# A fused attention and expert kernel on one core: both ends of the attention part re-ordered, and VectorE's first state difference put ahead of the mask of the first scores in every quad

## The reference, cut to what matters

```
xn = layernorm(x)
q, k, v = split(xn @ W_qkv)              # 16 heads of width 8; k is normalised per head
for each chunk of 64 tokens:
    inter  = S applied to q              # S is an 8 x 8 state per head and sequence
    scores = causal_mask(q k^T)          # 64 x 64 per head
    y      = inter + scores @ v
    S      = S + v^T k
out = x + y @ W_o + ffn(xn)              # ffn: the expert with the largest affinity, gated
```

## Time and profile before

| what | value |
|---|---|
| three runs | 389.06, 389.95, 390.57 us; median 389.95 |
| the profiled execution | 390.6 us, its span 388.9 us |
| mean granted TensorE clock | 0.987 of full speed |
| TensorE matmul busy | 357.8 us, 92% of the span |
| TensorE weight load busy | 300.1 us, 77% |
| VectorE, ScalarE, GpSimd busy | 288.6, 241.9, 251.4 us |
| attention part | 0 to about 243 us |
| expert part | from there to the end |

### The profile page before, as it was taken

The page is one execution under the profiler, slowest core; times in us unless marked ns, Lnnn a source line. Parts: engine busy times, 40 slices in busy tenths (PEclk is TensorE's granted clock), DMA queues, the critical chain, the costliest instruction groups (busy, mean ns, idle before and its releaser), DMA issues.

```text
span 388.9 us, 17635 instructions
## 1 busy us (share of the span) xinstructions
PE 357.8 (92%) x6900; PEld 300.1 (77%) x6900; DVE 288.6 (74%) x802; ACT 241.9 (62%) x657; POOL 251.4 (65%) x245
## 2 busy tenths in 40 slices
PE   7799999999999898999899988999999999999991
PEld 6477776766766666667567567899999999999990
DVE  8897895995966776857668458688888778877770
ACT  4788766766856556536545362666677676666760
POOL 3486757887875745445454350288888888888884
PEclk9999999999999999999999899999999999999996
DMA  6223153274022022443423423555555555555330
GB/s 193 56 57 83 35 166 111 79 227 138 10 78 78 25 86 70 106 149 98 132 67 109 139 63 79 136 70 74 69 72 68 72 67 73 72 72 71 35 28 0
DMA packets 55153, 33.18 MB, mean 85 GB/s; under 512 B 5352, under 2 KB 52768, under 8 KB 55072
## 3 DMA queue, kind: packets, MB, share of 16 engines
q1 hardware_dynamic: 42800, 23.53, 22.0%
q0 software_dynamic: 12272, 8.54, 15.7%
HBM read 18.72 MB, written 13.78 MB: 84 GB/s over the span
## 4 chain that ended last, share of the span: by engine, by line
PE 52%; issue 28%; POOL 12%; DVE 4%; ACT 2%; POOLq 1%; ACTq 0%; DVEq 0%
PE sc L1260 12%; POOL out_dram L494 12%; PE bank L1312 10%; PE bank L1321 4%; PE bank L1209 4%; PE bank L1196 4%; PE bank L1187 3%; PE bank L1292 2%; PE bank L1281 2%; PE bank L1241 2%; PE bank L1202 2%; PE bank L1153 2%; PE bank L1215 1%; PE bank L1220 1%; PE bank L1164 1%
## 5 line engine op out<-in xcount | busy, mean ns | idle before, releaser
L494 POOL DMA_INDIRECT out_dram<-qx,rows x71 | 112.8, 1588 | 35.7 <-issue 21.9
L694 ACT ACTIVATE qx<-sc,b1T 128x128 f32<-128x128 f32 x280 | 80.1, 369 | 40.1 <-PE sc L1405 32.6
L420 POOL DMA_INDIRECT slots_d<-rows,pos_i x64 | 63.6, 995 | 63.7 <-PE sc L1260 22.5
L852 DVE TENSOR_TENSOR pr<-sc,causal 128x1536 f32<-128x1536 f32 (+1 forms) x32 | 63.5, 1986 | 39.8 <-PE sc L1260 39.8
L1413 PE MATMUL bank<-tokens,qx 128*128 128x128 f32 x568 | 75.2, 275 | 0.7 <-ACT qx L694 0.7
L1405 PE MATMUL sc<-wide,tokens 128*128 128x128 f32 x560 | 74.0, 275 | 0.1
L1413 PEld LDWEIGHTS bank<-tokens,qx 128*128 128x128 f32 x568 | 69.0, 192 | 1.1 <-ACT qx L694 1.1
L1405 PEld LDWEIGHTS sc<-wide,tokens 128*128 128x128 f32 x560 | 68.1, 192 | 0.3 <-issue 0.3
L1260 PE MATMUL sc<-qx,kT 32*64 32x128 f32 x2048 | 52.5, 280 | 9.2 <-issue 8.8
L1260 PEld LDWEIGHTS sc<-qx,kT 32*64 32x64 f32 x2048 | 36.9, 130 | 31.1 <-issue 30.8
L1009 DVE COPY tokens<-xT 128x1024 f32 x71 | 56.0, 790 | 0.1
(11 more groups left out here) (167 smaller groups left out, 539.9 us busy)
## 6 DMA issues: line engine op xcount, KB each, us to landing
rows<-slots_d SPq DMA_DIRECT2D x71, 66.0 KB, 2.6
res<-in_L_attn_x_dram SPq DMA_DIRECT2D x16, 256.0 KB
out_dram<-res SPq DMA_DIRECT2D x16, 256.0 KB
tokens<-in_L_attn_x_dram SPq DMA_DIRECT2D x7, 512.0 KB, 4.1
w1raw<-in_L_ffn_w_dram SPq DMA_DIRECT2D x8, 256.0 KB
w2raw<-in_L_ffn_w_dram SPq DMA_DIRECT2D x8, 256.0 KB
out_dram<-qx,rows POOLq DMA_INDIRECT x71
slots_d<-rows,pos_i POOLq DMA_INDIRECT x64
```

What stands on the lines that cost most here:

```text
L420: pool.indirect_dma_start(slots_d, bass.IndirectOffsetOnAxis(ap=pos_i[:, t:t + 1], axis=0), rows[:, t, :], None, bounds_check=E * RT * P - ...
L494: pool.indirect_dma_start(out_rows, bass.IndirectOffsetOnAxis(ap=xs[:, a, D + 2:D + 3].bitcast(U32), axis=0), ye[:, a, :], None, bounds_ch ...
L694: last = nc.scalar.activation(ht[:, k % 2, c * P:(c + 1) * P], inner(k)[:, c * P:(c + 1) * P], ACT.Relu, bias=b1T[:, bass.ds(e * FC + c, 1)])
L852: nc.vector.tensor_tensor(pr[:, h % 2, a:G, :].rearrange("p g (j t) -> p (g j) t", t=CH), sc[:, a * BANK:G * BANK].rearrange("p (j t) -> p ...
```

## The change

1. **In the quads 1 to 15** VectorE takes the first difference, then the mask of the even half, then the second difference. Before, it took the mask, the first, the second.
2. **In quad 0** it takes both differences and the normalisation of its tile for a later step, then the mask; three small table operations move behind the mask. Ahead of that, four of the row statistics of step 2 come before `kT_copy(0)`, and `ln_moments(2)` before `k_var(0)`. ScalarE copies the transposed keys of quad 1 (`kT_copy(1)`) ahead of `values_across(0)`.
3. **At the end**, the second difference and the state's last sum of quads 14 and 15 are left out, on TensorE (half of `state_step`), on VectorE, and as a wait; nothing reads them. In quad 15 `b1_fold(7)` comes ahead of the first difference, the mask of half 31 is done in two halves, one per tile, with a wait between the products of the two tiles, and the weights' copies of the first two slots come ahead of those slots' scaling.

```diff
@@ ScalarE @@
             q_copy(0)
+            kT_copy(1)
             values_across(0)
...
                 if h % 2 == 0:
-                    if more:
+                    if n and more:
                         kT_copy(n + 1)
@@ VectorE, score_mask @@
-                nc.vector.tensor_tensor(pr[:, h % 2, a:G, :].rearrange("p g (j t) -> p (g j) t", t=CH),
-                                        sc[:, a * BANK:G * BANK].rearrange("p (j t) -> p j t", t=CH),
-                                        bcast(causal[:, :], 1, (G - a) * PAIR * TW // CH), ALU.mult).then_inc(s("so_sb"), 1)
+                for b in range(PAIR if h == NH - 1 else 1):
+                    w = slice(b * TW, (b + 1) * TW) if h == NH - 1 else slice(0, PAIR * TW)
+                    j = (w.stop - w.start) // CH
+                    nc.vector.tensor_tensor(pr[:, h % 2, a:G, w].rearrange("p g (j t) -> p g j t", t=CH),
+                                            sc[:, a * BANK:G * BANK].rearrange("p (g w) -> p g w", w=BANK)[:, :, w]
+                                            .rearrange("p g (j t) -> p g j t", t=CH),
+                                            bcast(bcast(causal[:, :], 1, j), 1, G - a), ALU.mult).then_inc(s("so_sb"), 1)
@@ VectorE, state_steps @@
-                dve.wait_ge(s("smid_ready"), n + 1)
-                dve.wait_ge(s("dstb_sb"), n + 1)
-                reach(dve, s("intera_ps"), n - 1)
-                nc.vector.tensor_tensor(st, smid[:, :, :], dstate[:, 1, :, :], ALU.add).then_inc(s("state_ready"), 1)
+                if n < NQ - 2:
+                    dve.wait_ge(s("smid_ready"), n + 1)
+                    dve.wait_ge(s("dstb_sb"), n + 1)
+                    reach(dve, s("intera_ps"), n - 1)
+                    nc.vector.tensor_tensor(st, smid[:, :, :], dstate[:, 1, :, :], ALU.add).then_inc(s("state_ready"), 1)
@@ VectorE, the program @@
+            ln_stats(2, range(4))
             kT_copy(0)
-            ln_stats(2, range(4))
+            ln_stats(2, range(4, B))
             kn_copy(0)
-            ln_stats(2, range(4, B))
+            ln_moments(2)
             k_var(0)
-            ln_moments(2)
...
                 if h % 2 == 0:
-                    score_mask(h)
-                    dstate_first(n)
-                    dstate_second(n)
+                    if n == 0:
+                        dstate_first(n)
+                        dstate_second(n)
+                        ln_inverse(2)
+                        ln_shift(2)
+                        ln_norm(2, (7,))
+                        score_mask(h)
...
+                    elif n == NQ - 1:
+                        b1_fold(E - 1)
+                        dstate_first(n)
+                        score_mask(h)
+                    else:
+                        dstate_first(n)
+                        score_mask(h)
+                    if n and n < NQ - 2:
+                        dstate_second(n)
...
-                        se_scale(0)
-                        se_scale(1)
                         dve.wait_ge(s("w1_sb"), E)
                         dve.wait_ge(s("w2_sb"), E)
                         se_weights(0, e[2])
                         se_weights(1, e[3])
+                        se_scale(0)
+                        se_scale(1)
@@ TensorE @@
                 if n:
-                    pe.wait_ge(s("dstb_sb"), n)
+                    pe.wait_ge(s("dstb_sb"), min(n, NQ - 2))
...
-                        for c, bank in ((0, Y[n % 2]), (1, FA)):
+                        for c, bank in ((0, Y[n % 2]), (1, FA))[:2 if n < NQ - 2 else 1]:
...
                     i = h % 2 * PAIR + b
+                    if b and h == NH - 1:
+                        pe.wait_ge(s("so_sb"), NH + 1)
```

More of the change, by code:

```diff
@@ L1026, in se_result @@
                                                op1=ALU.add).then_inc(s("ye_ready"), 1)
+            ln_stats(2, range(4))
             kT_copy(0)
-            ln_stats(2, range(4))
+            ln_stats(2, range(4, B))
             kn_copy(0)
-            ln_stats(2, range(4, B))
+            ln_moments(2)
             k_var(0)
-            ln_moments(2)
             k_rstd(0)
             v_scale(0, Y[1])
-            nc.vector.tensor_scalar(notbefore[:, :], ones_v[:, :], 1.0, None, ALU.subtract)
-            nc.vector.tensor_copy(iotk[:, :], iot_i[:, :])
-            nc.vector.tensor_copy(rows[:, :, D + 2].bitcast(I32), id_i[:, :])
             for h in range(NH):
@@ L1044, in _ @@
                 if h % 2 == 0:
-                    score_mask(h)
-                    dstate_first(n)
-                    dstate_second(n)
+                    if n == 0:
[5 more added lines that the diff above has]
+                        score_mask(h)
+                        nc.vector.tensor_scalar(notbefore[:, :], ones_v[:, :], 1.0, None, ALU.subtract)
+                        nc.vector.tensor_copy(iotk[:, :], iot_i[:, :])
+                        nc.vector.tensor_copy(rows[:, :, D + 2].bitcast(I32), id_i[:, :])
+                    elif n == NQ - 1:
[7 more added lines that the diff above has]
+                        dstate_second(n)
                     if n in (3, 5, 7, 9):
@@ L1051, in _ @@
                         state_steps(n)
-                    if norm:
+                    if n and norm:
                         ln_inverse(n + 2)
@@ L1074, in _ @@
                         result(n - 1)
-                    if n >= 8:
+                    if n >= 8 and n + 1 < NQ:
                         b1_fold(n - 8)
@@ L1423, in _ @@
             pe.wait_ge(s("w1_sb"), E)
-            pe.wait_ge(s("dstb_sb"), NQ)
             se_up(0)
```

## The result

The changed kernel takes **399.51 us** (median of 4 runs, 398.66 to 400.19), the kernel before in the same comparison 389.63 (4 runs, 389.06 to 390.57): ratio 1.0251, 95% interval 1.0216 to 1.0285. It is slower by 9.9 us. The prediction was 399.0 us, between 394 and 403. The profiled execution took 400.19 us, its span is 398.5 us where it was 388.9.

What follows compares the result with a forecast made beforehand. TensorE was taken to bound the kernel, with VectorE mostly waiting for it. The terms 4.4 + 1.9 + 0.6 + 3.0 - 0.6 + 0.7 - 1.0 sum to +9.0 us, giving a median of 399.0 us, range 394.0 to 403.0.

Steps and rivals of the forecast that it cites:

- quads 0 and 1: Start: quad 0's mask, behind differences and normalisation meeting GpSimd's mask, delays half 1's scores, +0.7 us; quad 1 has slack.
- quads 2, 4, 6: Late q_project (+0.4), late v_scale for the transposes (+0.2), VectorE meeting GpSimd's sum (+0.4): +1.0 us each, +3.0 in all.
- quad 3: inter_first no longer waits 0.59 us for the first difference, which now comes first: -0.6 us.
- quad 5: Has slack enough for the shift of VectorE's work: no cost.
- quads 7, 8: Shorter mask and longer TensorE halt, cost between nothing and quad 11's price: +0.6 us for both.
- quad 9: q_project waits for the ranks behind the second difference, +1.4 us, and FB's transpose for v_scale, +0.5: together +1.9.
- quads 10 to 13: VectorE starts 0.5 us after state_step, so q_project waits 1.1 us for the second difference in each: +4.4 us.
- quads 14, 15: Half of state_step left out in each, last products' wait for the mask gone, slots' work nearer: -1.0 us in all.
- expert part: The stretch after attention, with TensorE busy 134 of 142 us, stays as long as before.
- halts swallow the wait: Rival: from quad 7 on, TensorE's unnamed halts give way to the new wait; 392 to 396.5 us, chance 0.20.
- The long delay: Rival: VectorE sees state_step's end 1.5 us late in quads 9 to 13; 404.0 us, chance 0.07 for over 402.5.
- a gain: Rival: TensorE reaches q_project after the second difference even in the new order, leaving only gains; 387.5 us, chance 0.04.

Runs made afterwards that it cites:

- the run with the end alone: Kernel before with only part 3 of the change, the mask of quad 15 ahead of its difference: 391.87 us, ratio 1.0024.
- other work ahead: Kernel before; in quads 10 to 13 slots' places and b1_fold moved into VectorE's idle time, then first difference, mask, second difference: 392.75 us, ratio 1.0087.
- the run with the ends alone: Changed kernel with the kernel before's order (mask, first difference, second difference) in quads 1 to 15, both ends still changed: 365.59 us, ratio 1.0002.

## Why the prediction was right

By the quads' lengths (start of even scores to the next, in us): the first pair is the traces that the prediction was made from and judged by, the second the two of chip B.

| part | forecast | first pair | chip B |
|---|---|---|---|
| quads 0 and 1 | +0.7 | +1.2 | +0.3 |
| quads 2, 4, 6 | +3.0 | +2.3 | +2.0 |
| quad 3 | -0.6 | +0.3 | +0.3 |
| quad 5 | 0 | +0.3 | -0.3 |
| quads 7, 8 | +0.6 | +1.4 | +1.4 |
| quad 9 | +1.9 | +1.8 | +2.0 |
| quads 10 to 13 | +4.4 | +3.8 | +3.7 |
| quads 14, 15 | -1.0 | -1.9 | -1.1 |
| expert part | 0 | +0.3 | 0 |
| sum | 9.0 | 9.6 | 8.4 |

The rows are rounded. Stretches at 1.2 GHz are in them, each worth about 1 us: in quad 0 after and quad 14 before in the first pair, in quad 10 before on B.

- **Quads 10 to 13, right.** Both inputs came out: a delay of 0.58 us against 0.5, and the wait of 1.00 against 1.1 in quads 10 to 13. (By its own rows the prediction's wait is 176.70 - 175.66 = 1.04; what it has too much there it lacks in the price, as a bracket of 1.00 costs 1.16.) The quads 11 to 13 are each 1.1 to 1.3 us longer. Quad 10 has the wait too, but the kernel before had lost time there already, in the first trace to longer halts (its scores and products take 8.7 us there, those of the changed kernel 7.9), on B to the slow clock. Alone, these quads cost +5.3 and +5.0 us in the runs, within 0.9 of the term.
- **Quad 9, right in sum:** a wait of 1.48 for the ranks where 1.4 was worked out, which costs 1.6 to 1.7 us at the start of `q_project`. Of the 0.5 that `v_scale` was to cost at the end of the quad only 0.2 came.
- **Quads 2, 4, 6, nearly.** The parts are there. `q_project` waits 0.32 us in quad 4 where 0.4 was forecast, the transposes 0.17 for 0.2, and in quad 2 `ln_shift` meets GpSimd's sum as I had feared. But quad 6 lost nothing, though `q_project` waits 0.28 us in it, for which no term of mine says why; the halts lie at other places of it than before. On B quads 4 to 6 also win back the waits of `inter_first` that the kernel before had there. In the changed kernel's trace of chip B `ln_shift` in quad 2 is the first of these rows, GpSimd's sum the second:

```profile
44.86 0.69 DVE L781 SCALAR_TENSOR_TENSOR nmr<-mv,rstd 128x8 f32<-128x8 f32 x1
...
44.80 0.73 POOL L442 TENSOR_TENSOR state<-smid,dstate 128x256 f32<-128x256 f32 x1 [1.27 <-DVE dstate L871]
```

- **Quad 3, wrong by 0.9.** "Quad 3 gives something back": the wait of `inter_first` did go, and TensorE is 0.39 us ahead of its old place by the scores of the odd half. But the routing's eight matmuls behind them then take 1.78 us instead of 1.04, and the quad ends 0.3 later (before, then changed):

```profile
60.45 1.04 PE L1164 MATMUL bank<-xT,smallT 128*32 128x512 f32 x8
```
```profile
62.76 1.78 PE L1186 MATMUL bank<-xT,smallT 128*32 128x512 f32 x8
```

  I let a wait that vanished count as time, without asking what came next. What holds these matmuls no row names.
- **Quads 7 and 8, too low** (1.4 for 0.6): I took them between nothing and quad 11's price, and they lie nearer to that price. In quad 8 it is the wait of 0.52 at `q_project`. In quad 7 TensorE waits for no other engine; the odd half's scores, unbroken in 1.21 us before, now take 2.8 with halts, and the products 1.1 instead of 2.1. Why the halts moved is open.
- **Quad 0, right in mechanism.** `ln_shift` took 0.60 us and the normalisation 0.47, together what I had for the two, and the scores began at 20.57. I put the meeting on the normalisation (0.86) and it fell on the shift, which began at 17.77 and ended at 18.37, with GpSimd's mask:

```profile
17.07 1.27 POOL L412 TENSOR_TENSOR pr<-pr,causal 128x512 f32<-128x512 f32 x1
```

  The Trainium skill ("SBUF — State Buffer", "Who interferes with whom") says that a VectorE instruction with two SBUF inputs contends with a GpSimd instruction that reads SBUF, and that the order of issue decides which of the two is held. Both inputs of the shift lie in SBUF, GpSimd's mask had started first, and the shift ended 0.03 us after it: the trace agrees. The row that the prediction rested on fits less well, since there the normalisation (18.93) had started 0.05 us ahead of GpSimd's sum (18.98) and still took 0.86. What I missed: on B half 2 starts 1.1 us late and quad 2 only 0.3, as a halt of 0.9 us in quad 1 is gone. Here a halt did swallow a delay, in one place.
- **The end, right in the traces, not in the times:** 1.1 us on B, and 1.9 in the first pair, where the slow stretch in quad 14 before makes up about 1.2; the run with the end alone showed no gain.
- **The rivals.** That halts swallow the wait is refuted for quads 10 to 13 by chip A and D: with few halts and with many, the order there costs the same 5 us. One quad, with other work ahead (quad 12 on B), shows that it can happen. The long delay did not come in quads 9 to 13; it is 1.4 us in quads 7 and 8, as it was in quad 7 before. Nothing speaks for a gain.

The forecast was also lucky: in the first pair its parts were too low by 2.8 us together (0.9 in quad 3, 0.8 in 7 and 8, the rest in quads 0, 1 and 5 and the expert part) and too high by 2.3 (0.9 in quads 14 and 15, 0.7 in 2, 4 and 6, 0.6 in 10 to 13, 0.1 in quad 9), and that cancelled in the sum. The claim that VectorE's later work "is not hurt" in quads 10 to 13 is true on the chips with halts and false on chip A.

## What to carry to other kernels

Idle time ahead of an instruction is slack only for what is behind it in the queue: an instruction that waits for a later event, put ahead of one whose input is ready, gives that idle time away, and the other engine pays where it next needs the queue. Follow the displaced work through the queue to every consumer until the loop closes, not only to the first: with both differences first on chip A one wait of TensorE went and another took its place. And measure on more than one chip: which consumer waits can differ between two chips that agree in the total.

## What the runs showed of the hardware

**Chips differ by 6 to 7% here.** The kernel before took 366.08 us on A and 388.79 to 392.03 on the other three. The mean granted clock does not tell them apart: 0.989 to 0.995 in the runs on A, 0.984 to 0.995 on B. TensorE's halts without a named cause make a large part of the difference. Its waits in the run with the ends alone (A) and with quads 10 to 13 (D), in us, times, longest:

```profile
PE bank L1337 <- issue: 2.6, 5, 1.4
...
PE sc L1283 <- issue: 1.3, 1, 1.3
```
```profile
PE sc L1264 <- issue: 7.9, 28, 0.4
PE bank L1316 <- issue: 6.4, 15, 0.6
```

On D the even half's scores break at nearly the same places in quads 11 to 15, after 45 or 46, 4, and 5 or 6 matmuls. Quad 11, where they take 3.29 us from first to last; on A they take 1.21:

```profile
169.53 1.06 PE L1264 MATMUL sc<-qx,kT 32*64 32x128 f32 x46
170.87 0.45 PE L1264 MATMUL sc<-qx,kT 32*64 32x128 f32 x4 [0.28 <-issue]
171.58 0.45 PE L1264 MATMUL sc<-qx,kT 32*64 32x128 f32 x5 [0.26 <-issue]
172.31 0.51 PE L1264 MATMUL sc<-qx,kT 32*64 32x128 f32 x9 [0.28 <-issue]
```

On A quad 10 in the order of the kernel before takes 12.26 us, on B the quads 11 to 13 take 15.2. What holds TensorE back on three chips and not on the fourth is open; no run here tells.

**The granted clock** fell to 1.2 GHz for some 3 to 7 us ahead of the expert part, at changing places, in ten of the fourteen traces and not at all there in the other four. Ahead of the fall in quad 10 on B TensorE waited for no other engine, though its work was broken by halts. Two traces can differ by 1.2 us in a quad for that alone, so a clock row belongs beside every comparison of two quads.
